# Moving the weight rewrite behind the prefix loop, and loading the prefix rows in bf16 on the other DMA queue

## What is computed

```python
def attn(x):                      # x is already layer-normed
    z = x @ W.T
    m = scan(m * lam[k] + z)      # over rows, four decays lam[k]
    h = z + sum_k m[..., k] * eta[k]
    return gamma * layernorm(h) + beta
x = x + attn(layernorm(x))
y = fwht(layernorm(x) * SU_ug) / 64
v = silu(y @ W_gate.T * (Ws_gate * 64)) * (y @ W_up.T * (Ws_up * 64))
x = x + (fwht(v * SU_dp) / 64) @ W_down.T * (Ws_dp * 64)
```

## Time and profile before

| what | value |
|---|---|
| median of 13 runs | 7086.75 us (7000.93 to 7368.9) |
| profiled execution | 7007.35 us, span of its slowest core 7005.8 us |
| spans of the 8 cores | 6978.9 to 7005.8 us |
| PE busy | 3490.9 us, 50% of the span |
| DVE busy | 2442.4 us, 35% |
| ACT busy | 955.4 us, 14% |
| POOL busy | 161.6 us, 2% |
| bytes moved by q1 and q0 | 520.70 MB and 109.08 MB |

### The profile page before, as it was taken

One profiled execution on the slowest core, in us unless ns is written; L12 is line 12 of the kernel. 1 busy time (PEld: TensorE's weight loads), 2 busy tenths in 40 slices (PEclk: granted clock), 3 DMA queues, 4 the chain that ended last, 5 costly groups with the idle time before them and its releaser, 6 DMA issues.

```text
span 7005.8 us, 50263 instructions; the slowest of 8 cores (6978.9 to 7005.8 us)
## 1 busy us (share of the span) xinstructions
PE 3490.9 (50%) x16543; PEld 1517.0 (22%) x16543; DVE 2442.4 (35%) x2879; ACT 955.4 (14%) x2027; POOL 161.6 (2%) x311
## 2 busy tenths in 40 slices
PE   0000000125665119999999999412111296574844
PEld 0000000011221003444444444100000042232311
DVE  0112667644444651111111111343553433232322
ACT  0001344332111222000000000112111100000000
POOL 1000000000000000000000000000000011010100
PEclk9999999956776558999999999655555598787967
DMA  9999544321111111111122111132113365555553
GB/s 110 114 127 152 165 156 156 126 72 54 60 60 60 42 60 36 56 58 55 55 63 61 55 58 55 33 89 56 48 48 95 85 180 122 150 132 143 141 138 87
DMA packets 413912, 632.99 MB, mean 90 GB/s; under 512 B 34201, under 2 KB 329693, under 8 KB 389085
## 3 DMA queue, kind: packets, MB, share of 16 engines
q1 hardware_dynamic: 371838, 520.70, 23.9%
q0 software_dynamic: 41824, 109.08, 12.6%
HBM read 638.05 MB, written 167.77 MB: 115 GB/s over the span
## 4 chain that ended last, share of the span: by engine, by line
PE 44%; DVE 23%; DMA 9%; another core or an unknown queue 7%; issue 7%; ACT 5%; SPq 4%; DVEq 1%; ACTq 0%; POOL 0%; POOLq 0%
PE pd L1098 13%; PE pu L869 13%; PE pg L876 13%; DVE statc L211 4%; DMA ep<-x_dram 4%; DVE vq L966 3%; DVE btmp L964 3%; PE pz L601 2%; DMA G<-xfull 2%; SPq L935 2%; DVE vq L968 2%; ACT vq L948 1%; PE pq L944 1%; SPq L983 1%
## 5 line engine op out<-in xcount | busy, mean ns | idle before, releaser
L1098 PE MATMUL pd<-wdsl,v2sl 128*128 128x512 bf16 x4096 | 905.5, 384 | 433.4 <-DMA v2sl<-v_dram 362.8
L869 PE MATMUL pu<-uT_s,wslab 128*128 128x512 bf16 x4096 | 906.9, 380 | 0.8 <-ACT uT_s L818 0.8
L876 PE MATMUL pg<-uT_s,gslab 128*128 128x512 bf16 x4096 | 904.9, 379 | 0.0
L891 DVE SCALAR_TENSOR_TENSOR vtmp<-pu,wsupT,silb 128x1024 f32<-128x1024 f32 x128 | 164.3, 1284 | 1550.7 <-ACT silb L885 1550.7
L1098 PEld LDWEIGHTS pd<-wdsl,v2sl 128*128 128x128 bf16 x4096 | 402.5, 99 | 936.5 <-issue 470.0
L944 PE MATMUL pq<-vq,h_s 128*128 128x256 bf16 x512 | 182.2, 372 | 844.3 <-DMA vq<-v_dram 757.8
L1106 DVE TENSOR_TENSOR acc<-acc,pd 128x512 f32<-128x512 f32 x512 | 352.3, 688 | 643.0 <-PE pd L1098 643.0
L423 PE MATMUL pp<-w4b,H 128*128 128x4 bf16 x1792 | 63.4, 166 | 1004.0 <-DVE H L415 1004.0
L869 PEld LDWEIGHTS pu<-uT_s,wslab 128*128 128x128 bf16 x4096 | 400.9, 98 | 486.2 <-issue 4.0
L876 PEld LDWEIGHTS pg<-uT_s,gslab 128*128 128x128 bf16 x4096 | 401.1, 98 | 482.9
L964 DVE TENSOR_TENSOR btmp<-vq 128x8192 bf16<-128x8192 bf16 x48 | 212.4, 4425 | 547.2 <-ACT vq L948 542.7
(11 more groups left out here) (137 smaller groups left out, 2015.1 us busy)
## 6 DMA issues: line engine op xcount, KB each, us to landing
v2sl<-v_dram SPq DMA_DIRECT2D x256, 512.0 KB, 10.9
G<-xfull SPq DMA_DIRECT2D x112, 1024.0 KB, 5.9
wup_bf<-wupT POOLq DMA_DIRECT2D x16, 2048.0 KB, 165.5
wgate_bf<-wgateT POOLq DMA_DIRECT2D x16, 2048.0 KB, 484.3
G<-xown SPq DMA_DIRECT2D x32, 1024.0 KB, 6.6
wslab<-wup_bf SPq DMA_DIRECT2D x512, 64.0 KB, 2.0
gslab<-wgate_bf SPq DMA_DIRECT2D x512, 64.0 KB, 2.0
v_dram<-vchB SPq DMA_DIRECT2D x64, 512.0 KB, 2.7
```

What stands on the lines that cost most here:

```text
L869: last = pe.matmul(pu[par][:, s * 512:(s + 1) * 512], wslab[w % 2][:, c * 256 + jj * 128: c * 256 + (jj + 1) * 128], uT_s[:, c * T + hh * ...
L876: last = pe.matmul(pg[par][:, s * 512:(s + 1) * 512], gslab[w % 2][:, c * 256 + jj * 128: c * 256 + (jj + 1) * 128], uT_s[:, c * T + hh * ...
L891: m_stt_prev = DV.emit(lambda dv, jc=jc, par=par: dv.scalar_tensor_tensor(vtmp2[:, :], pu[par][:, :], wsupT[:, jc:jc + 1], silb2[:, :], AL ...
L1098: last = pe.matmul(pd[par][:, :], v2sl[sp_][:, jj * T + tch * 128: jj * T + (tch + 1) * 128], wdsl[sp_][:, jj * 512:(jj + 1) * 512], start ...
```

## The change

Three things are done.

- The 32 weight DMAs (`GPW`) and the 16 loads of `wzT_s` (`GPZ`) are emitted to POOL's queue behind the prefix loop, `wzT_s` first. The two loads of gamma and beta stay ahead of the loop.
- The prefix rows are loaded by POOL's queue, converted to bf16 on the way, into three slots of `xlnT_s`, which is not yet in use (slots of 2048 columns). The load of turn jp waits until ACT has squared the rows of turn jp-3 and DVE has written their centred copy.
- The sums, squares and the centred copy read these bf16 slots; the centred copy goes to two more slots of `xlnT_s`, from which PE multiplies. The statistics code that was a helper now stands in the loop itself, in the same order of steps.

```diff
@@ -232,13 +234,6 @@
-        for c in range(DC):
-            GPW.emit(lambda gp, c=c: gp.dma_start(
-                out=wup_bf[c * 128:(c + 1) * 128, :], in_=wupT[c * 128:(c + 1) * 128, :]))
-        for c in range(DC):
-            GPW.emit(lambda gp, c=c: gp.dma_start(
-                out=wgate_bf[c * 128:(c + 1) * 128, :], in_=wgateT[c * 128:(c + 1) * 128, :]))
-        m_gp_upgate = GPW.n
@@ -368,72 +363,6 @@
-            if jp >= 2:
-                SY.wait(DV, m_prep_ac[jp - 2])
-            SY.wait(DV, m_dvc)
-            m_ld = SYG[b].emit(lambda sy, jp=jp, b=b: sy.dma_start(
-                out=G[b][:, :], in_=xfull[jp * 128:(jp + 1) * 128, :]))
...
-            mcast = DV.emit(lambda dv, b=b, sp=sp: dv.tensor_scalar(
-                Hh[b][:, :], G[b][:, :], statc[:, sp + 1:sp + 2], None, ALU.add))
@@ -444,14 +373,118 @@
+        GPB.emit(lambda gp: gp.dma_start(out=gam_b[0:1, :], in_=gammain[:, :]))
+        GPB.emit(lambda gp: gp.dma_start(out=bet_b[0:1, :], in_=betain[:, :]))
...
+            if jp >= 3:
+                GP.wait(AC, m_prep_ac[jp - 3])
+                GP.wait(DV, m_prep_dv[jp - 3])
+            GPX3[b3].emit(lambda gp, jp=jp, b3=b3: gp.dma_start(
+                out=xlnT_s[:, b3 * D:(b3 + 1) * D],
+                in_=xfull[jp * 128:(jp + 1) * 128, :]))
...
+            DV.wait(GPX3[b3], m_ld)
...
+            DV.emit(lambda dv, b3=b3, sp=sp: dv.reduce_sum(
+                statc[:, sp:sp + 1], xlnT_s[:, b3 * D:(b3 + 1) * D], axis=AX.X))
...
+            mss = AC.emit(lambda ac, b3=b3, sp=sp: ac.activation(
+                zbf[:, :], xlnT_s[:, b3 * D:(b3 + 1) * D], AF.Square,
+                accum_out=statc[:, sp + 2:sp + 3]))
...
+            mcast = DV.emit(lambda dv, b3=b3, b=b, sp=sp: dv.tensor_scalar(
+                xlnT_s[:, (3 + b) * D:(4 + b) * D],
+                xlnT_s[:, b3 * D:(b3 + 1) * D],
+                statc[:, sp + 1:sp + 2], None, ALU.add))
...
         for c in range(DC):
             GPZ.emit(lambda gp, c=c: gp.dma_start(
                 out=wzT_s[:, c * D:(c + 1) * D], in_=wzT[c * 128:(c + 1) * 128, :]))
...
+        for c in range(DC):
+            GPW.emit(lambda gp, c=c: gp.dma_start(
+                out=wup_bf[c * 128:(c + 1) * 128, :], in_=wupT[c * 128:(c + 1) * 128, :]))
```

More of the change, by code:

```diff
@@ L141, in build_nc @@
     GPB = SubQ(GP)
+    GPX3 = [SubQ(GP) for _ in range(3)]
     SUBS = [SYG[0], SYG[1], SYX2, SYW[0], SYW[1], SYV[0], SYV[1],
@@ L144, in build_nc @@
             SYSL2[0], SYSL2[1], GPD2[0], GPD2[1],
-            SYE[0], SYE[1], SYY[0], SYY[1], SYR, GPW, GPZ, GPB]
+            SYE[0], SYE[1], SYY[0], SYY[1], SYR, GPW, GPZ, GPB,
+            GPX3[0], GPX3[1], GPX3[2]]
     with contextlib.ExitStack() as top:
@@ L369, in build_nc @@
         m_coefs = DV.n
+        stA = contextlib.ExitStack()
+        _open_stacks.append(stA)
+        wzT_s = stA.enter_context(nc.sbuf_tensor("wzT_s", [128, DC * D], BF16))
+        xlnT_s = stA.enter_context(nc.sbuf_tensor("xlnT_s", [128, DC * T], BF16))
+        gam_b = stA.enter_context(nc.sbuf_tensor("gam_b", [128, D], BF16))
+        bet_b = stA.enter_context(nc.sbuf_tensor("bet_b", [128, D], BF16))
+        zbf = stA.enter_context(nc.sbuf_tensor("zbf", [128, D], BF16))
+        hb = stA.enter_context(nc.sbuf_tensor("hb", [128, D], F32))
+        Hh = [stA.enter_context(nc.sbuf_tensor(f"H{i}", [128, D], BF16)) for i in range(2)]
+        GPB.emit(lambda gp: gp.dma_start(out=gam_b[0:1, :], in_=gammain[:, :]))
+        GPB.emit(lambda gp: gp.dma_start(out=bet_b[0:1, :], in_=betain[:, :]))
+        m_gb = GPB.n
         if kphase < 2:
@@ L378, in build_nc @@
         for jp in range(PREV):
+            b3 = jp % 3
             b = jp % 2
-            if jp >= 2:
-                SY.wait(DV, m_prep_ac[jp - 2])
-            SY.wait(DV, m_dvc)
-            m_ld = SYG[b].emit(lambda sy, jp=jp, b=b: sy.dma_start(
-                out=G[b][:, :], in_=xfull[jp * 128:(jp + 1) * 128, :]))
-            m_prep_ld.append(m_ld)
-            sp = 8 * (jp % 2)
-            AC.wait(SYG[b], m_ld)
+            sp = 8 * (jp % 2)
+            if jp >= 3:
+                GP.wait(AC, m_prep_ac[jp - 3])
+                GP.wait(DV, m_prep_dv[jp - 3])
@@ new lines, in build_nc @@
+            GPX3[b3].emit(lambda gp, jp=jp, b3=b3: gp.dma_start(
+                out=xlnT_s[:, b3 * D:(b3 + 1) * D],
+                in_=xfull[jp * 128:(jp + 1) * 128, :]))
+            m_ld = GPX3[b3].n
+            m_prep_ld.append(m_ld)
+            if jp >= 2:
+                DV.wait(DV, m_prep_dv[jp - 2])
+            DV.wait(GPX3[b3], m_ld)
+            if jp == 0:
+                DV.wait(DV, m_coefs)
+            DV.emit(lambda dv, b3=b3, sp=sp: dv.reduce_sum(
+                statc[:, sp:sp + 1], xlnT_s[:, b3 * D:(b3 + 1) * D], axis=AX.X))
@@ L388, in build_nc @@
+            DV.wait(DV, DV.n)
+            DV.emit(lambda dv, sp=sp: dv.tensor_scalar_mul(statc[:, sp + 1:sp + 2],
+                                                           statc[:, sp:sp + 1], -1.0 / D))
+            AC.wait(GPX3[b3], m_ld)
+            AC.wait(AC, AC.n)
             if jp >= 2:
                 AC.wait(DV, m_prep_dv[jp - 2])
[L390 to L393, removed]
@@ L394, in build_nc @@
-            mvar, mrs = emit_stats(lambda b=b: G[b][:, :], lambda: zbf[:, :], sp,
-                                   extra_dv_wait=edw)
+            mss = AC.emit(lambda ac, b3=b3, sp=sp: ac.activation(
+                zbf[:, :], xlnT_s[:, b3 * D:(b3 + 1) * D], AF.Square,
+                accum_out=statc[:, sp + 2:sp + 3]))
+            m_prep_ac.append(mss)
+            DV.wait(AC, mss)
+            DV.emit(lambda dv, sp=sp: dv.tensor_scalar_mul(statc[:, sp + 3:sp + 4],
+                                                           statc[:, sp + 2:sp + 3], 1.0 / D))
@@ new lines, in build_nc @@
+            DV.wait(DV, DV.n)
+            DV.emit(lambda dv, sp=sp: dv.tensor_mul(statc[:, sp + 5:sp + 6],
+                                                    statc[:, sp + 1:sp + 2], statc[:, sp + 1:sp + 2]))
+            DV.wait(DV, DV.n)
+            mvar = DV.emit(lambda dv, sp=sp: dv.tensor_sub(
+                statc[:, sp + 3:sp + 4], statc[:, sp + 3:sp + 4], statc[:, sp + 5:sp + 6]))
+            AC.wait(DV, mvar)
+            AC.emit(lambda ac, sp=sp: ac.activation(statc[:, sp + 4:sp + 5], statc[:, sp + 3:sp + 4],
+                                                    AF.Ln, bias=consts[:, 0:1]))
@@ L396, in build_nc @@
+            AC.wait(AC, AC.n)
+            mrs = AC.emit(lambda ac, sp=sp: ac.activation(statc[:, sp + 4:sp + 5], statc[:, sp + 4:sp + 5],
+                                                          AF.Exp, scale=consts[:, 2:3]))
             DV.wait(AC, mrs)
@@ L410, in build_nc @@
                 w4b[b][:, :], w4f[:, :], pmask_s[:, jp:jp + 1], None, ALU.mult))
-            m_prep_dv.append(mw4)
             DV.wait(DV, mw4)
@@ L414, in build_nc @@
                 DV.wait(PE, m_prep_pe[jp - 2])
-            mcast = DV.emit(lambda dv, b=b, sp=sp: dv.tensor_scalar(
-                Hh[b][:, :], G[b][:, :], statc[:, sp + 1:sp + 2], None, ALU.add))
-            m_prep_ac.append(mcast)
+            mcast = DV.emit(lambda dv, b3=b3, b=b, sp=sp: dv.tensor_scalar(
+                xlnT_s[:, (3 + b) * D:(4 + b) * D],
+                xlnT_s[:, b3 * D:(b3 + 1) * D],
+                statc[:, sp + 1:sp + 2], None, ALU.add))
+            m_prep_dv.append(mcast)
             PE.wait(DV, mcast)
@@ L421, in pmm @@
                 last = None
+                xc0 = (3 + b) * D
                 for c in range(DC):
                     last = pe.matmul(pp2[:, 4 * c:4 * c + 4],
-                                     Hh[b][:, c * 128:(c + 1) * 128],
+                                     xlnT_s[:, xc0 + c * 128: xc0 + (c + 1) * 128],
                                      w4b[b][:, :],
@@ L430, in build_nc @@
             m_prep_pe.append(m_pe)
+        for c in range(DC):
+            GPZ.emit(lambda gp, c=c: gp.dma_start(
+                out=wzT_s[:, c * D:(c + 1) * D], in_=wzT[c * 128:(c + 1) * 128, :]))
+        m_gp_wz = GPZ.n
+        for c in range(DC):
+            GPW.emit(lambda gp, c=c: gp.dma_start(
+                out=wup_bf[c * 128:(c + 1) * 128, :], in_=wupT[c * 128:(c + 1) * 128, :]))
+        for c in range(DC):
+            GPW.emit(lambda gp, c=c: gp.dma_start(
+                out=wgate_bf[c * 128:(c + 1) * 128, :], in_=wgateT[c * 128:(c + 1) * 128, :]))
+        m_gp_upgate = GPW.n
         DV.wait(PE, m_prep_pe[-1])
@@ L436, in build_nc @@
             return nc
[L437 to L453, removed]
         PE.wait(GPB, m_gb)
```

## The result

The changed kernel took 6940.6 us in the median of 11 runs (6826.98 to 7288.64), against 7128.61 for the kernel before in 48 runs; the ratio is 0.972, with a 95% interval of 0.968 to 0.977. 0.972 of the profiled execution's 7007.35 us is 6812, where 6820 was forecast.

A forecast was written before the change was run, and what follows sets the result against it. POOL's weight rewrite starves SP's loads, then DVE's chain bounds the loop. Start -288, first to last reduce -335, to A0's load +26, A0 +389: 208 us off 7007.35 gives 6799; forecast 6820, range 6740 to 6940.

The forecast's parts named there:

- Start: Before the prefix loop: constants take 10 us instead of 234, so the first reduce stands at 57 us.
- Turn: Prefix loop: the bf16 centred copy takes 750 ns instead of 1286, so a turn takes 6.2 us instead of 6.75.
- Rival 1: Prefix loop: the 16-bit copy brings nothing, turns stay at 6.75 us, +61, 6860 from the profile; chance 0.11.
- POOL's queue: Prefix loop: loads 3.0 to 4.9 us apart suffice; a latency of 10.1 us is hidden within 12.4 by three slots.
- rivals 2 and 4: Prefix loop: POOL's loads late, either slower overall (latency beyond 18 us, chance 0.06) or turns of 7.4 us, 6932 (0.06).
- W: Before the state's matmuls: the sixteen loads of wzT_s land at 790 us, some 38 us behind the loop's end at 752.
- A0 beside the rewrite: Phase A0: SP's 16 loads meet the rewrite's packets at 38.2 us each; A0 takes 628 us instead of 239.
- rival 3: A0 into A1: the rewrite moves 80 MB per ms instead of 99, ends at 1629, time 6894; chance 0.09.
- All behind it stays: From A1's first matmul (1439 us, 1647.40 before) to the end: unchanged, so the whole is 208 us less.
- the prediction's own sign: Phase A1: turns longer than before would show the prediction wrong.
- the rewrite's tail: Phase A1: the rewrite runs 26 us into it, covered by two pz groups of 9.6 us and the statistics; costs nothing.
- The level: Whole kernel: 6799 us off the profiled execution, 6878 off the median; 6820 forecast, nearer the former; forecast's chance 0.66.

## Why the prediction was right

- *Start.* 57 us forecast, 62.7 measured. The constants have landed at 17.66 instead of 10, which more than covers the difference.
- *Turn.* 6.2 forecast, 6.20 measured: the centred copy takes 754 ns (750 taken), the reduce 2279 (no gain taken). Rival 1 falls. The Trainium skill, VectorE: DVE Perf Modes, in the perf-mode tier table, has 693 ns for the copy; the 754 measured stand 61 above it, as the float32 form's 1286 stood 59 above its 1227. That the reduce has one speed agrees.
- *POOL's queue.* The rate sufficed. The latency was the mis-sized term: 10.1 us by adding up 64 KB, 4 KB and 1 MB rows, where the loads landed in 5.1 us, 6.7 beside a paced rewrite. The one-row load of 4 KB that I built on is no measure of a load of 128 rows, nor of POOL's queue: the two such loads at the start of the changed kernel (gamma, beta) landed in 2.3 and 3.4 us, not in 6.2. The error cost nothing in the sum, since 10.1 was hidden too, but it kept rivals 2 and 4 alive; with two slots the turn stayed at 6.21, and they fall. Nor does any row show loads held back by DVE, which spent 84.4 of the 688 us in the centred copy and was busy for 467.9 in all: the trap of the Trainium skill, SBUF — State Buffer, section on the two separate sides, cost nothing that can be seen here.
- *W.* Landed at 795.3 (790), A0's first load at 816.0 (811): the 5 us of the start, carried along.
- *A0 beside the rewrite.* 37.9 us a turn (38.2) and 53.91 MB in 540 us, 99.8 MB per ms (99). The last rewrite DMA landed near 1462 (1465), so rival 3 falls. This was the largest term, and the row of the prefix loop could be carried over because the same two queues sent the same packets. That two loads were always out was not so: 14 x 57.7/540 = 1.5 in the mean, against 7 x 70.5/267 = 1.85 in the prefix loop before, and the loads still came 38 us apart.
- *A1 begins* at 1444.25 (1439): every step up to here was right within 6 us, but for the constants' 8.
- *"All behind it stays"* is the step that failed: 17 us were lost behind A1's begin on core 4, and by the prediction's own sign (A1's turns longer than before) it was wrong there. A1's 13 are not the rewrite's tail, which was priced at nothing: the turns are longer up to the last one, and with two slots the tail ends at the same time and core 4's A1 takes 584 us. They are 8 us of stores that land later and 5 us of products, at a granted clock of 0.70 instead of 0.73, means between the levels of 1.2 and 2.4 GHz. Why the stores land later in some executions on some cores, and what sets that clock, was not tried. The clock alone doesn't separate the cores: in the run with two slots core 5 took 584 us at 0.71 and core 6 took 600 at 0.72. B2's 11 us, at the same clock of 0.50 and with the same instructions, are no sure effect of the change either: between the first second-transform matmul and the first of the down product lie 1115 to 1122 us on the eight cores before, 1127 to 1131 on cores 4 to 7 after, and 1124 to 1127 on cores 0 to 3 with the slices alone, where nothing was moved. Their cause stays open.
- *The level.* I took the profiled execution rather than the median. The fastest four runs lie there (6826.98 to 6837.56); the median of 6940.6 is at the edge of the range, 0.6 us over the 6940 named. That 6820 came so near is in part luck: the terms gave 6799, and the 21 us added towards the median happened to be about what was lost behind A1's begin.

What the prediction didn't see is that the change was only a third of what could be had. It priced the rewrite per packet, and rightly, but took the packet as given. By medians over undisturbed cores of one profile each, the kernel before spans 6991 us and the changed one 6818; slices of 2048 columns alone give 6813, slices and move together 6559, and with the pacing it is 6476.

## What to carry to other kernels

When a bulk transfer on one DMA queue starves another queue, look at its packets before its place: compare both queues' packet counts and shares in the stretch, and if the counts are equal and the shares are not, try slicing the transfer. Then move it to where the other queue asks for least, and let it trickle through a stretch bound by an engine (here 687 us of DVE chain with half the DMA time free). A slowdown measured beside one stretch could be carried to another here, 38.2 to 37.9 us, where both queues sent the same packets; that 1.85 loads were out in the mean in the one and 1.5 in the other made no difference.

## What the runs showed of the hardware

- SP's and POOL's queues sent packets one for one (2058 to 2060) although the packets hold an engine for 3.65 and 0.54 us in the mean. With slices the counts are not equal (3226 to 2005 and 6280 to 2193); then SP had only 14 x 15.5/260 = 0.8 loads out in the mean, against 14 x 57.7/540 = 1.5, so its queue was empty for part of the time. That doesn't explain all: with the slices in the kernel before, 70 x 15.2/790 = 1.35 loads were out, and the counts were 16370 to 10206. Why they differ with small packets stays open.
- A load of 128 rows on POOL's queue, converted on the way, landed in 5.1 us in the median, no later than SP's float32 load, and over 112 turns DVE's reduces waited 0.1 us for such loads.
- Sixteen loads of W and 40 slices could be paced through the loop, whose DMA share was then 0.92: the prefix loads landed in 6.7 instead of 5.1 us on core 0 (8.6 on core 4), and the turn stayed at 6.20.
